# Global attention in blocks of 256 queries instead of halves of 512

## The chip, the cores and the metric

One NeuronCore of a Trainium2 chip runs the whole program, and the other cores are idle. The metric is the device time of one execution in microseconds (us). An execution works through four batches of 1024 tokens one after the other, in one hardware loop of which the body is the same for each batch. Of the engines, TensorE (PE) multiplies and transposes, VectorE (DVE) and ScalarE (ACT) do elementwise work and reductions, GpSimd (POOL) helps, and SyncE (SP) mainly issues DMAs. Every engine takes its instructions in order, and the engines meet at semaphores.

## The reference, cut to what matters

The model has two layers. The change touches only the global attention of the second one, `_L1_attn_ref`, with 1024 tokens, 16 heads and a head width of 8:

```python
Q, K, V = (proj(Wq, bq), proj(Wk, bk), proj(Wv, bv))     # 4 x 16 x 1024 x 8
logits = jnp.einsum('bhqd,bhkd->bhqk', Q, K) / scale * scale_matrix
attn = jax.nn.softmax(logits, axis=-1)
out = jnp.einsum('bhqk,bhkd->bhqd', attn, V) * (1.0 + yellow * eps_adaptive)
out = out.transpose(0, 2, 1, 3).reshape(B, S, d) @ Wo.T + bo
```

Before it stand the first layer (a kernel attention with cumulative sums and a mixture of experts), and after it a stack of two local attentions with feed-forward parts. These are the same in both kernels.

## The kernel before, in words

**Operands.** The 16 heads form four groups of four. `QS` and `KS` hold queries and keys of a group in bf16 pieces, 48 rows per head, so that a bf16 product gives nearly the fp32 product. A head of a group has a number `j = 2 s + r`: `r` says in which half of the partitions (from 0 or from 64) it lies, `s` is an index. Two products with different `r` run side by side on PE. Two further rows of `QS` (50 in all) hold the maximum of each query's scores, in two bf16 pieces, against rows of -1 in `KS`, so that the product of 50 rows gives score minus maximum.

**Two streams.** The maxima come first, from products of their own. A "maximum" is one product of 128 queries by 512 keys into one bank of PSUM (`maxima`, L1350 by the helper `mm`), which DVE reduces to a column (L1105). A half is 512 queries of one group: it has 4 query tiles x 2 key halves x 4 heads = `MPH` = 32 maxima, and there are `HALVES` = 8 halves, so 256 maxima for a batch. When the 32 of a half are done, DVE joins them to 16 columns in `mtop` (L1110), PE transposes these ("mT", L1584), ACT copies the rows to `mrw` (`rows_out`, L650), POOL splits them into two pieces `msp` (L475, L477), SP writes them to DRAM (`load_max`, L375) and, when that has landed, reads them into `QS` with two DMAs (L380).

The second stream has 128 steps `n` for a batch. Two steps make a unit of 512 queries by 128 keys; step `n` takes the pair of heads `s = n % 2`. In a step PE does two products of 128 keys by 512 queries, side by side (`st_ps`), ACT takes the exponential of 128x1024 in one instruction (L658), and three steps later PE multiplies `vaug` (values and a 1 for the denominator) with the exponentials in four products of 256 columns. These collect in bank 4. After 16 steps a half is complete, and ACT copies bank 4 to `on` (L669), at `n = 16 (h + 1) + 2` for half `h`. PE doesn't begin the next half's value products before that copy.

**How they are woven.** PE's order is written out: ahead of step `n` it issues the maxima up to number `ahead(n + 1)`, where `ahead(n) = 38 + 2 n + min(2 (n // 3), 8)`. So a step has two maxima, and four steps early on have four. The maxima and transposes share a ring of banks: all eight for the first 32, then banks 5, 6 and 7, each free again when DVE (for an mT: ACT) has read it. The transpose of half `h` stands behind the second maximum of the half after it; for the first and last half directly behind its own. At `n = 16 h` PE waits for the row of half `h` (`m_row`).

**SP's order.** SP does `load_max(h)` for h = 0 to 7. Between these it loads the operands of the groups (`load_group`) and moves the finished output of a group away (`move_out(g)`): eight DMAs of 32 KB from `on` to `o_t` and `den_t` (L387, L388), which wait for both copies to `on` of the group. `move_out(0)` stands behind `load_max(3)`, `move_out(1)` behind `load_max(5)`, `move_out(2)` ahead of `load_max(7)`. The first copy to `on` of group g waits on ACT until all eight moves of group g-1 have landed (`act.wait_ge(S["on_moved"], 128 * g)`, L668), since it writes over what they read.

Of the kernel before, what the change touches and what calls it, by code (L numbers as in the profile page):

```python
# [14 lines left out]
P = 128  # L15
# [19 lines left out]
UNITS = HALVES * T  # L35
MPH = 32
AHEAD = MPH + 6
CATCH_UP = 8
# [19 lines left out]
def build(nc, d, out):  # L58

    with ExitStack() as ctx:  # L60
# [135 lines left out]
        mxp = take([2, GH, T // 2, 2])  # L196
        mtop = take([2, MPH // 2])
# [41 lines left out]
        xa xaT_ps xaT q_ps k_ps v1_ps qkf bf1 r1 bf2 bf3 vaug scr_w0 scr_w1 qs_early qs_loaded0 qs_loaded1 qs_loaded2 qs_loaded3 mx_ps mx mtop mT_ps mrw msp m_scr m_row  # L239
# [49 lines left out]
        def max_of(h, n):  # L289

            if h == 0:
                return n // 4 % 4, n // 16, n // 2 % 2
            return n // 8, n // 2 % 2, n // 4 % 2

        def ring_bank(kind, h, n):

            i = ring_at[kind, h, n]
            return i % 8 if i < MPH else 5 + i % 3
# [6 lines left out]
        def ahead(n):  # L305

            return AHEAD + 2 * n + min(2 * (n // 3), CATCH_UP)
# [19 lines left out]
        def _(sp):  # L327
# [13 lines left out]
            with sp.Fori(0, B) as b:  # L341
# [28 lines left out]
                def load_max(h):  # L370
                    g, hq = h // 2, h % 2
                    sp.wait_ge(S["msp"], 2 * (h + 1))
                    if h >= 2:
                        sp.wait_ge(S["m_row"], 32 * h)
                    sp.dma_start(scr_m[h % 2].rearrange("i (r c) -> r i c", c=P), msp[0:MPH // 2, h % 2])\  # L375
                        .then_inc(S["m_scr"], 16)
                    sp.wait_ge(S["m_scr"], 16 * (h + 1))
                    rows = scr_m[h % 2].rearrange("i (s r n) -> r i s n", r=2, n=HALF)
                    for r in range(2):
                        sp.dma_start(QS[64 * r + STACK:64 * r + STACK + PIECES_M, g, :, HALF * hq:HALF * hq + HALF],  # L380
                                     rows[r]).then_inc(S["m_row"], 16)

                def move_out(g):
                    sp.wait_ge(S["on"], 2 * g + 2)
                    for j in range(GH):
# [56 lines left out]
        def _(pool):  # L442
            with pool.Fori(0, B) as b:
# [26 lines left out]
                for h in range(HALVES):  # L470
                    rows = slice(0, MPH // 2)
                    pool.wait_ge(S["mrw"], h + 1)
                    if h >= 2:
                        pool.wait_ge(S["m_scr"], 16 * (h - 1))
                    pool.tensor_copy(msp[rows, h % 2, 0], mrw[rows, h % 2]).then_inc(S["msp"], 1)  # L475
                    pool.wait_ge(S["msp"], 2 * h + 1)
                    pool.tensor_tensor(msp[rows, h % 2, 1], mrw[rows, h % 2], msp[rows, h % 2, 0], ALU.subtract)\  # L477
# [36 lines left out]
        def _(act):  # L514
# [18 lines left out]
            with act.Fori(0, B) as b:  # L533
# [110 lines left out]
                def rows_out(h):  # L644

                    rows = slice(0, MPH // 2)
                    act.wait_ge(S["mT_ps"], h + 1)
                    if h >= 2:
                        act.wait_ge(S["msp"], 2 * (h - 1))
                    act.copy(mrw[rows, h % 2], PS[rows, ring_bank("mT", h, 0), 0:P]).then_inc(S["mrw"], 1)  # L650

                rows_out(0)
                for n in range(2 * UNITS + 3):
                    if n < 2 * UNITS:
                        act.wait_ge(S["st_ps"], n + 1)
                        if n >= 8:
                            act.wait_ge(S["pv"], n // 2 - 3)
                        act.activation(pb[:, n % 8], pair(2 * (n % 2)), ACT.Exp).then_inc(S["p"], 1)  # L658
                        for h in range(1, HALVES):
                            last = MPH * (h + 1) + (1 if h < HALVES - 1 else -1)  # L660
                            if ahead(n) <= last < ahead(n + 1):
                                rows_out(h)
                    if n >= 16 and n % 16 == 2:
                        h = n // 16 - 1
                        g, hq = h // 2, h % 2
                        act.wait_ge(S["pv"], T * (h + 1))
# [90 lines left out]
        def _(dve):  # L757
# [128 lines left out]
            with dve.Fori(0, B) as b:  # L886
# [213 lines left out]
                for h in range(HALVES):  # L1100
                    for n in range(MPH):
                        t, hf, s = max_of(h, n)
                        j = 2 * s + n % 2
                        dve.wait_ge(S["mx_ps"], h * MPH + n + 1)
# [842 lines left out]
```

## Time and profile before

| | us |
|---|---|
| median of 3 runs | 2665.46 (2664.93 to 2665.88) |
| profiled execution, its own time | 2669.65 |
| profiled execution, span | 2667.9 |
| mean granted clock of TensorE in it | 0.913 |
| PE busy, 17520 matmuls | 2175.1 |
| DVE busy | 1967.1 |
| ACT busy | 1435.0 |
| POOL busy | 584.0 |

The profile is of one execution. Its own time is 1.75 us more than its span, for what lies around it, and 4.2 us more than the median. An engine's busy time is the sum over its instructions; for PE it is modelled, since matmuls are pipelined. A line of the view of instructions in order of time begins with the start in us from the span's start and the duration in us, then engine, line of the code, operation, output and input, and in square brackets the idle time of the engine before it and what ended it; x5 means that five such in a row are merged.
### The profile page before, as it was taken

The numbers are of one execution on the slowest core, as the hardware profiler recorded it, in microseconds if no ns is written. First come the engines' busy times: TensorE is split into PE (matmuls) and PEld (weight loads), VectorE is DVE, ScalarE is ACT, GpSimd is POOL, SyncE is SP. The second block draws the span as 40 slices with busy tenths as digits, with TensorE's granted clock in tenths as the row PEclk, the third lists the DMA queues.
The fourth block names the chain that finished last, engine by engine and source line by source line (L and its number), as shares of the span: only waits on it lengthen the run. The fifth ranks groups of instructions, "written<-read, shape, count | busy, mean of one in ns | idle before, by whom it ended". The sixth has DMA issues, their size and how long they took to land.

```text
span 2667.9 us, 46774 instructions
## 1 busy us (share of the span) xinstructions
PE 2175.1 (82%) x17520; PEld 1235.2 (46%) x17520; DVE 1967.1 (74%) x4192; ACT 1435.0 (54%) x2637; POOL 584.0 (22%) x400
## 2 busy tenths in 40 slices
PE   3799689878779959988779977997877995898777
PEld 3667312354647712246465741225564672223645
DVE  4865789678675589967777469967877657996677
ACT  1234267674733427766653335777473342776755
POOL 0062100124134200040405320004312531003050
PEclk9999779989879969999888987998987996999889
DMA  4000200011000020010100021001100003001010
GB/s 151 0 1 1 72 26 10 15 23 30 15 10 1 2 83 18 10 30 5 31 21 1 1 60 31 18 6 31 24 15 18 1 1 84 18 10 29 7 30 21
DMA packets 58920, 63.92 MB, mean 24 GB/s; under 512 B 17136, under 2 KB 44080, under 8 KB 58160
## 3 DMA queue, kind: packets, MB, share of 16 engines
q1 hardware_dynamic: 55480, 57.77, 8.6%
q8 instruction: 148, 2.42, 0.4%
q10 hardware_dynamic: 3192, 2.90, 0.3%
q14 instruction: 100, 0.82, 0.1%
HBM read 25.19 MB, written 15.01 MB: 15 GB/s over the span
## 4 chain that ended last, share of the span: by engine, by line
PE 47%; DVE 28%; ACT 14%; issue 6%; DMA 2%; SPq 2%; POOL 0%; DVEq 0%; ACTq 0%; POOLq 0%
PE PS L1350 44%; DVE arena L1105 10%; ACT arena L715 7%; DVE arena L1204 2%; ACT arena L658 1%; PE PS L1675 1%; DVE tmp L1179 1%; DVE s_at L1179 1%; DVE arena L1172 1%; PE PS L1368 1%; DMA tmp<-xf 1%; ACT tmp L669 1%; DVE arena L1291 1%; SPq L329 1%; ACT arena L723 1%
## 5 line engine op out<-in xcount | busy, mean ns | idle before, releaser
L1350 PE MATMUL PS<-arena 128*32 128x256 f32 (+4 forms) x10240 | 807.7, 349 | 132.7 <-DVE arena L1105 50.1
L1105 DVE TENSOR_REDUCE arena<-PS 128x1 f32<-128x512 f32 x1024 | 640.5, 685 | 41.1 <-PE PS L1350 41.1
L658 ACT ACTIVATE arena<-PS 128x1024 f32<-128x1024 f32 x512 | 517.9, 1028 | 174.1 <-PE PS L1350 173.0
L1350 PEld LDWEIGHTS PS<-arena 128*32 128x32 f32 (+4 forms) x10240 | 309.2, 121 | 626.0 <-DVE arena L1105 265.6
L610 ACT ACTIVATE arena<-PS 128x512 f32<-128x512 f32 x256 | 150.8, 597 | 244.2 <-PE PS L1350 244.0
L1350 PEld LDWEIGHTS PS<-w2e,arena 128*128 128x128 f32 x2048 | 246.0, 192 | 50.6 <-issue 49.8
L1350 PE MATMUL PS<-w2e,arena 128*128 128x128 f32 x2048 | 247.7, 275 | 0.3
L715 ACT ACTIVATE arena<-PS,arena 128x128 f32<-128x128 f32 x512 | 230.9, 546 | 22.3 <-DVE arena L1241 20.9
L1068 DVE TENSOR_TENSOR arena<-PS,arena 128x512 f32<-128x512 f32 x128 | 86.2, 689 | 208.5 <-PE PS L1350 208.1
L1350 PE MATMUL PS<-wqkv,arena 128*128 128x512 f32 x384 | 179.4, 607 | 25.5 <-ACT arena L697 21.7
L465 POOL TENSOR_TENSOR zz<-zz,arena 128x512 f32<-128x512 f32 x104 | 135.4, 1302 | 265.4 <-DVE arena L1068 236.6
L475 POOL CAST arena<-arena 16x128 bf16<-16x128 f32 x32 | 9.0, 280 | 699.0 <-ACT arena L650 699.0
L715 ACT ACTIVATION_READ_ACCUMULATOR arena<-PS,arena 128x1 f32 x512 | 149.7, 293 | 0.0
L454 POOL TENSOR_TENSOR arena<-arena 128x1024 f32<-128x1024 f32 x32 | 75.2, 2350 | 249.9 <-ACT arena L562 239.8
L1239 DVE TENSOR_REDUCE arena<-PS 128x8 f32<-128x1024 f32 x64 | 78.3, 1224 | 63.4 <-PE PS L1350 62.7
L502 POOL TENSOR_TENSOR tmp<-xf,b2f 128x1024 f32<-128x1024 f32 x8 | 18.8, 2355 | 471.1 <-ACT xT L735 471.1
L1350 PE MATMUL PS<-x,w1e 128*128 128x512 f32 x256 | 120.5, 596 | 0.1
L1350 PE MATMUL PS<-xT,w1e 128*128 128x512 f32 x256 | 120.5, 596 | 0.1
L1350 PEld LDWEIGHTS PS<-wqkv,arena 128*128 128x128 f32 x384 | 69.3, 193 | 104.6 <-issue 83.1
L1350 PE MATMUL PS<-xT,wf 128*128 128x512 f32 (+1 forms) x192 | 89.8, 597 | 3.8 <-ACT xT L735 3.8
L696 ACT ACTIVATE arena<-PS 128x1024 f32<-128x1024 f32 x32 | 32.8, 1024 | 103.8 <-DVE s_at L1179 103.8
L1350 PE MATMUL PS<-c_blk,arena 128*128 128x16 f32 x256 | 54.8, 374 | 41.0 <-ACT arena L523 41.0
(301 smaller groups left out, 3435.3 us busy)
## 6 DMA issues: line engine op xcount, KB each, us to landing
arena<-arena SPq DMA_DIRECT2D x120, 128.0 KB, 2.3
scr_q<-arena SPq DMA_DIRECT2D x40, 128.0 KB, 2.5
scr_k<-arena SPq DMA_DIRECT2D x40, 128.0 KB, 2.4
arena<-scr_k SPq DMA_DIRECT2D x24, 200.0 KB
arena<-scr_q SPq DMA_DIRECT2D x24, 192.0 KB
x_in<-in_x SPq DMA_DIRECT2D x5, 512.0 KB, 4.0
out_x<-tmp SPq DMA_DIRECT2D x4, 512.0 KB, 3.9
wqkv<-in_wqkv SPq DMA_DIRECT2D x1, 1536.0 KB, 7.1
```

What stands on the lines that cost most here:

```text
L454: pool.tensor_tensor(ub[:, c % 2], vsb[:, c % 2], bsb[:, c % 2], ALU.mult).then_inc(S["ub"], 1)
L465: pool.tensor_tensor(zz[:, half], src[:, half], ym[:, m % 4], ALU.add).then_inc(S["z"], 1)
L610: act.activation(hs[:, n % 8], PS[:, up_bank("up", k, c), :], ACT.Silu).then_inc(S["hs"], 1)
L658: act.activation(pb[:, n % 8], pair(2 * (n % 2)), ACT.Exp).then_inc(S["p"], 1)
L696: act.activation(qk_sq[l][t % 2], pair(2 * (t % 2)), ACT.Square).then_inc(S["sq"], 1)
L715: act.activation(pl[:, n % 3, r, c], PS[:, 2 * (n % 2) + r, KEYS * c:KEYS * c + KEYS], ACT.Exp, bias=ml[:, n % 2, r, c:c + 1], scale=rq[:, ...
L1068: dve.tensor_tensor(ym[:, m % 4], PS[:, 4 + m % 4, :].rearrange("p (t w) -> p t w", w=W), bc(comb[:, half, e // EPG, e % EPG], [P, T // 2, ...
L1105: dve.tensor_reduce(mxp[:, h % 2, j, t, hf:hf + 1], PS[:, ring_bank("mx", h, n), :], AX, ALU.max)\
L1179: ins = dve.tensor_tensor(o, v, bc(w, [P, 2, HL, DL // 2], 2), ALU.mult)
L1204: dve.tensor_reduce(ssq[:, k], qk_sq[l][k % 2].rearrange("p (h c) -> p h c", c=DL), AX, ALU.add).then_inc(S["ssq"], 1)
L1239: link(dve.tensor_reduce(ml[:, n % 2], sv, AX, ALU.max))
L1350: return pe.matmul(o, w, v, start=start, stop=stop, **kw)
```

## The change

A block of 256 queries of a group takes the place of the half. A batch has 16 blocks with 16 maxima each; number and form of the maxima are the same (256 of 128x512). The first 32 are interleaved: 16 for the first key half of blocks 0 and 1, then 8 that complete block 0, then 8 that complete block 1. Each block has its own transpose (8 columns instead of 16), copy, split and three DMAs, so 16 of each a batch instead of 8, and each block's transpose stands behind the second maximum of the block after it (only the last one directly behind its own).

A step is now one block by 128 keys for all four heads: PE does four products of 256 columns (two side by side for `s = 0`, then two for `s = 1`, all into the same two banks) instead of two products of 512 columns. ACT's exponential has the same form, and the value products are four of 256 columns as before. There are still 128 steps, and the copies to `on` stay at the same steps `n`. The run-ahead is constant: `ahead(n) = 34 + 2 n`.

On SP, `move_out` is cut in two: heads 0 and 1 of a group behind `load_max` of block 6, 10 and 13, heads 2 and 3 behind that of block 7, 11 and 14. ACT does the first two `rows_out` ahead of its first exponential. `load_group(2)` and `(3)` stand behind `load_max` of block 1 and 5. There are two semaphores `m_row0` and `m_row1` in turn.

The diff, cut to its core (constants, ring, SP, ACT, PE; in DVE's loop only the numbering and the place of L1110 follow):

```diff
-UNITS = HALVES * T
-MPH = 32
-AHEAD = MPH + 6
-CATCH_UP = 8
+BLOCKS = 2 * HALVES
+QB = HALF // 2
+STEPS = BLOCKS * T
+MPB = 2 * (QB // P) * GH
+MAXIMA = BLOCKS * MPB
+ROWS = GH * QB // P
+AHEAD = 2 * MPB + 2
...
+        def max_at(m):
+
+            if m < 2 * MPB:
+                return m // 8 % 2, m // 4 % 2, m // 2 % 2, m // MPB
+            return m // MPB, m // 8 % 2, m // 4 % 2, m // 2 % 2
+
+        def maxima_by(blk):
+
+            return (MPB + MPB // 2, 2 * MPB)[blk] if blk < 2 else MPB * (blk + 1)
+
+        def row_after(blk):
+
+            return maxima_by(blk) + (2 if blk < BLOCKS - 1 else 0)
+
+        row_at = {row_after(blk): blk for blk in range(BLOCKS)}
+
         ring = []
-        for h in range(HALVES):
-            for n in range(MPH):
-                ring.append(("mx", h, n))
-                if n == 1 and 2 <= h:
-                    ring.append(("mT", h - 1, 0))
-            if h == 0 or h == HALVES - 1:
-                ring.append(("mT", h, 0))
+        for m in range(MAXIMA):
+            ring.append(("mx", m))
+            if m + 1 in row_at:
+                ring.append(("mT", row_at[m + 1]))
...
         def ahead(n):
 
-            return AHEAD + 2 * n + min(2 * (n // 3), CATCH_UP)
+            return AHEAD + 2 * n
...
-                for h in range(HALVES):
-                    if h == HALVES - 1:
-                        move_out(NGRP - 2)
-                    load_max(h)
-                    if h in (0, 2):
-                        load_group(2 + h // 2)
-                    if h >= 3 and h % 2 == 1 and h < HALVES - 1:
-                        move_out((h - 3) // 2)
+                for blk in range(BLOCKS):
+                    load_max(blk)
+                    if blk in (1, 5):
+                        load_group(2 + blk // 4)
+                    if blk in (6, 10, 13):
+                        move_out((blk - 6) // 3, (0, 1))
+                    if blk in (7, 11, 14):
+                        move_out((blk - 7) // 3, (2, 3))
...
                 rows_out(0)
-                for n in range(2 * UNITS + 3):
-                    if n < 2 * UNITS:
+                rows_out(1)
+                for n in range(STEPS + 3):
+                    if n < STEPS:
                         act.wait_ge(S["st_ps"], n + 1)
                         if n >= 8:
-                            act.wait_ge(S["pv"], n // 2 - 3)
+                            act.wait_ge(S["pv"], n - 7)
                         act.activation(pb[:, n % 8], pair(2 * (n % 2)), ACT.Exp).then_inc(S["p"], 1)
-                        for h in range(1, HALVES):
-                            last = MPH * (h + 1) + (1 if h < HALVES - 1 else -1)
-                            if ahead(n) <= last < ahead(n + 1):
-                                rows_out(h)
+                        if ahead(n + 1) in row_at:
+                            rows_out(row_at[ahead(n + 1)])
...
-                        for r in range(2):
-                            rows = slice(64 * r, 64 * r + STACK + PIECES_M)
-                            ins = mm(PS[:, 2 * (n % 2) + r, :], KS[rows, g, st, P * kt:P * kt + P],
-                                     QS[rows, g, st, HALF * hq:HALF * hq + HALF], tile_position=(64 * r, 0))
+                        for s in range(2):
+                            for r in range(2):
+                                rows = slice(64 * r, 64 * r + STACK + PIECES_M)
+                                ins = mm(PS[:, 2 * (n % 2) + r, QB * s:QB * s + QB], KS[rows, g, s, P * kt:P * kt + P],
+                                         QS[rows, g, s, QB * q4:QB * q4 + QB], tile_position=(64 * r, 0),
+                                         skip_group_check=True)
                         ins.then_inc(S["st_ps"], 1)
```

## Rows read from the trace of the kernel before

**Rows 1.** The page: span, busy engines, chain that ended last.

```profile
span 2667.9 us, 46774 instructions
...
PE 2175.1 (82%) x17520; PEld 1235.2 (46%) x17520; DVE 1967.1 (74%) x4192; ACT 1435.0 (54%) x2637; POOL 584.0 (22%) x400
...
PE 47%; DVE 28%; ACT 14%; issue 6%; DMA 2%; SPq 2%; POOL 0%; DVEq 0%; ACTq 0%; POOLq 0%
```

**Rows 2.** Busy time by stretch, batch 1: the stage, then its even middle.

```profile
955.20:1153.60 198.40, 164.42 (x1557) 44.30 (x1556) 170.26 (x271) 135.09 (x146) 5.62 (x17) 0.91 0.11 27
...
989.30:1125.20 135.90, 120.53 (x1206) 31.84 (x1202) 129.85 (x212) 104.63 (x112) 4.19 (x12) 1.00 0.07 14
```

**Rows 3.** DVE in order of time, one half's maxima in the even middle.

```profile
403.21 0.19 DVE L1110 TENSOR_REDUCE arena<-arena 128x16 f32<-128x32 f32 x1
403.31 1.28 DVE L1105 TENSOR_REDUCE arena<-PS 128x1 f32<-128x512 f32 x2
405.15 12.52 DVE L1105 TENSOR_REDUCE arena<-PS 128x1 f32<-128x512 f32 x20 [0.56 <-PE PS L1350]
418.00 6.28 DVE L1105 TENSOR_REDUCE arena<-PS 128x1 f32<-128x512 f32 x10 [0.34 <-PE PS L1350]
424.32 0.19 DVE L1110 TENSOR_REDUCE arena<-arena 128x16 f32<-128x32 f32 x1
```

**Rows 4.** DVE, then ACT, in order of time: how batch 1 begins.

```profile
969.63 4.86 DVE L1105 TENSOR_REDUCE arena<-PS 128x1 f32<-128x512 f32 x8
974.52 0.18 DVE L1110 TENSOR_REDUCE arena<-arena 128x16 f32<-128x32 f32 x1
975.80 1.29 DVE L1105 TENSOR_REDUCE arena<-PS 128x1 f32<-128x512 f32 x2 [1.09 <-PE PS L1350]
...
981.04 2.06 ACT L658 ACTIVATE arena<-PS 128x1024 f32<-128x1024 f32 x2 [4.22 <-PE PS L1350]
...
988.42 1.02 ACT L658 ACTIVATE arena<-PS 128x1024 f32<-128x1024 f32 x1 [0.96 <-PE PS L1350]
```

**Rows 5.** PE, then ACT, in order of time, batch 1, behind the last maximum.

```profile
1125.56 0.27 PE L1584 MATMUL PS<-ident,arena 128*16 128x128 f32 x1 [1.67 <-DVE arena L1110]
...
1129.45 6.52 ACT L658 ACTIVATE arena<-PS 128x1024 f32<-128x1024 f32 x7 [0.48 <-PE PS L1350]
```

**Rows 6.** Busy time by stretch, batch 1, behind the last transpose.

```profile
1125.80:1129.20 3.40, 3.40 (x23) 0.67 (x22) 0.77 (x1) 2.18 (x3) 0.70 (x2) 0.50 0.00 0
```

**Rows 7.** DVE, ACT, then SP in order of time, batch 0, behind half 5.

```profile
445.43 0.19 DVE L1110 TENSOR_REDUCE arena<-arena 128x16 f32<-128x32 f32 x1
...
450.10 1.02 ACT L658 ACTIVATE arena<-PS 128x1024 f32<-128x1024 f32 x1 [0.22 <-PE PS L1350]
...
458.82 0.59 ACT L669 COPY tmp<-PS 128x512 f32<-128x512 f32 x1 [0.21 <-DMA tmp<-tmp]
...
448.43 0.31 SPq L375 DMA_DIRECT2D scr_m<-arena  x1
449.77 1.22 SPq L380 DMA_DIRECT2D arena<-scr_m  x2
451.03 0.68 SPq L387 DMA_DIRECT2D xT<-tmp  x1
...
453.12 0.62 SPq L388 DMA_DIRECT2D tmp<-tmp  x1
...
455.79 1.24 SPq L388 DMA_DIRECT2D tmp<-tmp  x1
```

**Rows 8.** SP's own waits in batch 0's stage: total, times, longest, in us.

```profile
SPq L380 <- DMA scr_m<-arena: 11.9, 8, 2.9
```

**Rows 9.** Weight port and PE in order of time, at the start of one step.

```profile
380.34 0.14 PEld L1350 LDWEIGHTS PS<-arena 48*128 48x128 bf16 x4 [0.52 <-DVE arena L1105]
380.37 0.61 PE L1350 MATMUL PS<-arena 48*128 48x512 bf16 x4
```

**Rows 10.** Groups of weight loads, batch 0's stage: those of the scores.

```profile
L1350 PEld LDWEIGHTS PS<-arena 50*128 50x128 bf16 x256 | 13.6, 95 | 11.2 <-ACT arena L658 7.4 <-issue 2.1 <-DMA arena<-scr_m 0.8
```

More of the change, by code:

```diff
@@ L368, in load_group, with load_max, move_out @@
                             .then_inc(S["qs_loaded%d" % g], 16)
[L370 to L378, printed above, removed]
+                def load_max(blk):
+                    g, q4 = blk // 4, blk % 4
+                    sp.wait_ge(S["msp"], 2 * (blk + 1))
+                    if blk >= 2:
+                        sp.wait_ge(S["m_row%d" % ((blk - 1) % 2)], 32 * ((blk + 1) // 2))
+                    maxes = scr_m[blk % 2][:, 0:GH * QB]
+                    sp.dma_start(maxes.rearrange("i (r c) -> r i c", c=P), msp[0:ROWS, blk % 2]).then_inc(S["m_scr"], 16)
+                    sp.wait_ge(S["m_scr"], 16 * (blk + 1))
+                    rows = maxes.rearrange("i (s r n) -> r i s n", r=2, n=QB)
                     for r in range(2):
-                        sp.dma_start(QS[64 * r + STACK:64 * r + STACK + PIECES_M, g, :, HALF * hq:HALF * hq + HALF],
-                                     rows[r]).then_inc(S["m_row"], 16)
-                def move_out(g):
+                        sp.dma_start(QS[64 * r + STACK:64 * r + STACK + PIECES_M, g, :, QB * q4:QB * q4 + QB],
+                                     rows[r]).then_inc(S["m_row%d" % (blk % 2)], 16)
+                def move_out(g, heads):
                     sp.wait_ge(S["on"], 2 * g + 2)
-                    for j in range(GH):
+                    for j in heads:
                         h = GH * g + j
@@ L468, in _ @@
                 pool.tensor_tensor(s1[:], xa[:], bc(res["bo"][:], [P, T, W], 1), ALU.add).then_inc(S["xab"], 1)
[L470 to L477, printed above, removed]
+                for blk in range(BLOCKS):
+                    rows = slice(0, ROWS)
+                    pool.wait_ge(S["mrw"], blk + 1)
+                    if blk >= 2:
+                        pool.wait_ge(S["m_scr"], 16 * (blk - 1))
+                    pool.tensor_copy(msp[rows, blk % 2, 0], mrw[rows, blk % 2]).then_inc(S["msp"], 1)
+                    pool.wait_ge(S["msp"], 2 * blk + 1)
+                    pool.tensor_tensor(msp[rows, blk % 2, 1], mrw[rows, blk % 2], msp[rows, blk % 2, 0], ALU.subtract)\
                         .then_inc(S["msp"], 1)
@@ L1553, in ring_free @@
                     if ring_last[i]:
-                        kind, h, n = ring_last[i]
-                        if kind == "mx":
-                            pe.wait_ge(S["mx"], MPH * h + n + 1)
-                        else:
-                            pe.wait_ge(S["mrw"], h + 1)
-                def maxima(lo, hi):
-                    for m in range(lo, min(hi, MPH * HALVES), 2):
-                        h, n = m // MPH, m % MPH
-                        g, hq = h // 2, h % 2
-                        t, hf, s = max_of(h, n)
-                        if h == 0 and n == 0:
+                        kind, n = ring_last[i]
@@ L1567, in maxima @@
+                        pe.wait_ge(S["mx" if kind == "mx" else "mrw"], n + 1)
+                def maxima(lo, hi):
+                    for m in range(lo, min(hi, MAXIMA), 2):
+                        blk, t, s, hf = max_at(m)
+                        g, q4 = blk // 4, blk % 4
+                        if m == 0:
                             pe.wait_ge(S["qs_early"], 16 * 4)
-                        if h == 0 and n == MPH // 2:
+                        if m == MPB:
                             pe.wait_ge(S["qs_loaded0"], 16 * 4)
-                        if n == 0 and hq == 0 and h:
+                        if m and m % (4 * MPB) == 0:
@@ L1605, in _ @@
                 maxima(0, ahead(0))
-                for n in range(2 * UNITS + 3):
-                    if n < 2 * UNITS:
-                        u, st = n // 2, n % 2
-                        h, kt = u // T, u % T
-                        g, hq = h // 2, h % 2
+                for n in range(STEPS + 3):
+                    if n < STEPS:
+                        blk, kt = n // T, n % T
+                        g, q4 = blk // 4, blk % 4
                         maxima(ahead(n), ahead(n + 1))
-                        if n % 16 == 0:
-                            pe.wait_ge(S["m_row"], 32 * (h + 1))
+                        if kt == 0:
+                            pe.wait_ge(S["m_row%d" % (blk % 2)], 32 * (blk // 2 + 1))
@@ new lines, in _ @@
+                        blk, k = (n - 3) // T, (n - 3) % T
+                        pe.wait_ge(S["p"], n - 2)
+                        if k == 0 and blk % 2 == 0 and blk:
+                            pe.wait_ge(S["on"], blk // 2)
+                        c0 = QB * (blk % 2)
+                        for j in range(GH):
+                            c = HALF * (j % 2) + QB * (j // 2)
+                            ins = mm(PS[32 * j:32 * j + 32, 4, c0:c0 + QB], vaug[:, k, GH * (blk // 4) + j],
+                                     pb[:, (n - 3) % 8, c:c + QB], start=(k == 0), stop=(k == T - 1),
+                                     tile_position=(0, 32 * j), skip_group_check=True)
@@ L1640, in _ @@
+                        ins.then_inc(S["pv"], 1)
                 pe.wait_ge(S["p"], NGRP * T * GH)
```

95 lines of the change are left out of this document (39 added, 56 removed).

## The prediction

> **What bounds the kernel now.** I read the page first. PE is busy 82% of the span and DVE 74%, and the chain that ended last is shared, 47% on PE and 28% on DVE [rows 1]: no one engine bounds the program, so the stage must be read by itself. The view by stretch gives the global attention of batch 1: 198.4 us, with DVE busy 170.3, PE 164.4 and ACT 135.1 [rows 2]. Four such stages are 0.3 of the span. In the order of time DVE runs its reductions without a gap for 20 in a row, 12.52 us or 0.626 each [rows 3]. So the even middle goes at DVE's pace, two maxima and one step in 1.25 us. ACT confirms it: its exponential takes 1.02 and it idles 0.22 before it [rows 7]; the weight port waits 0.52 for a reduction to free a bank [rows 9]. The stage has three parts with three limits:
>
> - The beginning. A row of maxima must be complete before the first exponential. From the join (L1110) at 974.52 to the first exponential at 981.04 are 6.5 us [rows 4]. PE is at half clock until 989.3: from there the granted clock is 1.00, and the beginning puts the stage's mean at 0.91 [rows 2]. A step with value products takes 1.02 + 0.96 = 1.98 us [rows 4]: PE bounds.
> - The middle, bound by DVE. One half takes 424.32 - 403.21 = 21.11 us, of which 32 x 0.626 = 20.03 are reductions. Of the other 1.08, 0.34 is an idle time at the copy to `on`, which leaves 0.74 for join and transpose (0.56 of it idle) [rows 3].
> - The end. `ahead` reaches 256 at n = 105, so the maxima are all issued with step 104, and 24 steps go without them, bound by ACT: 6.52 / 7 = 0.93 us a step [rows 5].
>
> So a change gains in the middle only if DVE loses fewer microseconds.
>
> **The change, part by part, for one batch.**
>
> *The earlier first row.* Block 0 is complete after 24 maxima, 8 sooner. Eight take 4.86 us [rows 4], so its join is at about 969.7 on batch 1's clock, and its row is there by 975.5. But PE's order puts the transpose of block 1 ahead of step 0, and that needs 32 maxima. DVE has by then paid one more gap (1.09 is the row [rows 4]; 0.7, since two maxima stand behind the transpose here) and goes at the cold pace of 1.45 us a pair (from 975.80, two reductions and 0.17 idle), so the 32nd ends at 976.0, the 34th at 977.4, and the first exponential comes at about 978.7: 2.3 us sooner. ACT's table load moves behind the second `rows_out` and still ends before that.
>
> *The run-ahead without catch-up.* The early steps of before have four maxima at times, which keeps DVE busier while PE is cold. Followed pair by pair, the new kernel has issued 46 maxima where the old has issued 48 (986.4), though it is two steps further, and 54 against 54 at 991 to 992. So DVE's progress is the same, and the earlier start buys nothing at the end. I take 0, within 1.3 us (one pair) either way. It holds if the clock rises no later after the start than now.
>
> *More rows.* The middle has 13 transposes (blocks 2 to 14) for 6 (halves 1 to 6). Seven more at 0.74 [rows 3] are **+5.2 us**. Their geometry is the same: two maxima behind the block's last, ACT's copy behind the step's exponential. Bounds: 0.18 each if only the join remains (+1.3), 1.1 each as at the start (+7.7) [rows 4]. Each row now has nine steps from transpose to use instead of seven, so no row is late. The halved DMAs on SP fit between blocks that are 10 us apart.
>
> *The shorter end.* `ahead` is 256 at n = 111, so 18 steps instead of 24 go without maxima: 6 x 0.93 [rows 5] = **-5.6 us**. DVE's total is what it was, so that is a true gain. What DVE does behind the last row is asked for by PE only at n = 125, 14 steps later.
>
> *Four products for two.* PE streams the same columns, with two more weight loads a step. Their mean is 95 ns [rows 10]. Cost from below: nothing. From above: both exposed, 0.19 a step. Four loads, the two of the maxima and the two of the scores on the same partitions, pass in 0.14 us while the products that began at 380.37 still run [rows 9]. So I take hidden, 0.02 us on 12 cold steps, +0.2. The cover is PE's own idle time, (135.90 - 120.53) / 99 = 0.155 us a step in the middle [rows 2]; without it the excess counts 105 times.
> The Trainium skill (TensorE: Matmul & The Clock Gate, Part 3) says that a weight load overlaps running matmuls "only when row_grp differs"; the same page (Part 2) allows it for the background buffer too. The strict rule would expose the second pair; rows 9 speak against it.
>
> *The moves of the output.* This is the part that decides. The first copy to `on` of groups 1, 2 and 3 (n = 50, 82, 114) waits on ACT for all eight moves of the group before. Now four of these stand behind `load_max` of block 7, 11 and 14. The transpose of block 7 is issued in step 47 (34 + 2 x 47 = 128, and 130 is its place), that of block 11 in step 79, that of block 14 in step 103. So for groups 1 and 2 ACT needs the moves three steps after the transpose; for group 3 there are eleven steps, enough. Before, it was some nine steps, and even so the copy at 458.82 waited 0.21 us [rows 7].
> The time is in rows 7, with the join at 445.43 as zero. SP issues the write of the row at +3.00, the reads at +4.34, the first move at +5.60 and the fourth at +7.69. The last move lands and frees ACT 458.82 - 455.79 = 3.0 us after its issue begins (less the 0.6 by which that issue was held up: 2.4). So ACT is freed at +10.1 to +10.7. It would have copied behind the exponential of step 50, the third after the transpose's own: 450.10 and the pace of 0.93 [rows 5] give +5.60. The wait is 4.5 to 5.1 us; I take **4.6**, as a half's moves hold each other up less. Queued behind it on ACT is the exponential of step 51, and PE waits for the copy before the value products of step 51, with DVE's next maxima behind these. DVE has at most three banks and idles already at each copy [rows 3], so all of the wait passes to it, and the run-ahead, tied to n, never makes it up. Two a batch, eight in all: 8 x 4.6 = **+37 us**.
> Two additions. The write of the row takes up to 2.9 us to land instead of about 1.0 (8 waits sum to 11.9, so two of eight are long [rows 8]): two of the eight stalls are 1.9 longer, +4. And PE idles about 5 us in each. Ahead of the last transpose PE idled 1.7 us in batch 1 [rows 5], and then its clock was 0.50 for 3.4 us [rows 6]. A cold step costs 1.98 for 1.25, so 3.4 us of half clock cost 1.3 and twice that 2.5: I take 1.5 each, +12, from 0 to +20.
> [...]
>
> **The sum.** Beginning 0, rows +5.2, end -5.6, products +0.2: about 0 a batch, 0 in four. Stalls 37 + 4 + 12 = 53. The profiled execution would go from 2669.65 to about 2722; it stands 4.2 above the median, so the median goes from 2665.5 to **2718 us**. 0.2% or 5.3 us is about what a measurement of this kernel can tell from no change.
>
> **The rivals.**
>
> - *The moves arrive in time.* That needs 4.5 us less than rows 7 give for the same DMAs in the same order, or SP running ahead of the row, which its waits forbid. Then the sum is 0 and the time 2665, within 6. Against it also: the old order had three times the room and was just in time.
> - *Faster, by transposes that cost little.* If the joins fall into gaps that DVE has anyway, only 1.3 of 5.2 us remain a batch: 4 x -3.9 = -16, 2650. It decides only if the stalls together are under 16 us, 2 us each, less than half of the lowest bound. The lead in the exponentials (2.3 us) speaks for it, DVE's unbroken runs [rows 3] against.
> - *PE becomes the bound.* If the second pair of weight loads is exposed at 0.19 us a step, 0.155 is covered in the middle and 0.035 is not, x 105 = 3.7, and 0.19 x some 15 cold steps = 2.9; with the end's 18 steps partly touched, some 8 us a batch, +32: 2750.
> - *The stalls are shorter, the clock holds.* 8 x 4.0 and no additions: 2697.
>
> **Chances.** The forecast with its spread (2697 to 2748) 0.80; PE the bound 0.08 (on top of the stalls); in time 0.05; faster 0.03; something else slower 0.04. The range from below is 32 us of stalls less 4 for the beginnings, 2694; from above it is 8 x 5.1 + 15 (every write long) + 20 + 6 = 82, 2748. Slower by over 0.2% holds 0.92, within 0.2% 0.05, faster 0.03.
>
> **What would show each step right or wrong.** The copy L669 of the third and fifth half in each batch would show an idle time of 4 to 7 us ended by a DMA `tmp<-tmp`, and DVE an idle time of about 5 at the same place; the half that holds it lasts some 28 us from join to join instead of 21.9. Plain halves would last 21.9 (two joins). The first exponential would come some 2.7 us after block 1's join. The last maximum of a batch would end 5 + 13 us later than now, and 18 exponentials would follow it. Granted clock under 1.00 behind each stall would show the clock's part. Wrong would be: no wait at these copies, a steady step over 1.25 us (products), or a weight port that idles on "issue".

## The result, and the profile after

The changed kernel takes 2716.06 us (median of 4 runs, 2713.98 to 2717.45) against 2665.67 for the kernel before (4 runs, 2664.93 to 2666.13). The ratio is 1.0189, with a 95% interval from 1.0171 to 1.0206: 50 us or 1.9% slower. The profiled execution has a span of 2714.7 us against 2667.9, so 46.8 us more.

The page of the changed kernel, span, busy time, chain that ended last, and two groups of instructions; below them the same two groups of the kernel before:

```profile
span 2714.7 us, 49306 instructions
...
PE 2197.8 (81%) x18576; PEld 1287.8 (47%) x18576; DVE 1974.4 (73%) x4224; ACT 1443.1 (53%) x2669; POOL 605.8 (22%) x464
...
PE 44%; DVE 33%; ACT 12%; issue 6%; DMA 2%; SPq 2%; POOL 0%; DVEq 0%; ACTq 0%; POOLq 0%
...
L1113 DVE TENSOR_REDUCE arena<-PS 128x1 f32<-128x512 f32 x1024 | 644.0, 686 | 97.0 <-PE PS L1359 97.0
L669 ACT ACTIVATE arena<-PS 128x1024 f32<-128x1024 f32 x512 | 520.8, 1027 | 176.2 <-PE PS L1359 173.4
```

```profile
L1105 DVE TENSOR_REDUCE arena<-PS 128x1 f32<-128x512 f32 x1024 | 640.5, 685 | 41.1 <-PE PS L1350 41.1
L658 ACT ACTIVATE arena<-PS 128x1024 f32<-128x1024 f32 x512 | 517.9, 1028 | 174.1 <-PE PS L1350 173.0
```

DVE's work grew by 7 us only [rows 1]. What grew is its idle time ahead of the reductions: 97.0 us, where the kernel before has 41.1 in the same group. That is 56 us more of waiting for PE, in an engine that sets the pace of the middle.

The list of ACT's waits shows what made PE late. Total us, times and the longest, of the changed kernel and then of the kernel before:

```profile
ACT tmp L678 <- DMA tmp<-tmp: 28.3, 8, 3.6
...
ACT tmp L669 <- DMA tmp<-tmp: 0.9, 3, 0.4
```

Eight times a copy to `on` waits some 3.5 us for a move of the output, twice a batch. One of them, batch 1, in order of time: ACT, then DVE, then SP.

```profile
1050.29 1.02 ACT L669 ACTIVATE arena<-PS 128x1024 f32<-128x1024 f32 x1 [1.01 <-PE PS L1359]
1051.21 0.24 ACT L660 COPY arena<-PS 8x128 f32<-8x128 f32 x1
...
1053.99 1.02 ACT L669 ACTIVATE arena<-PS 128x1024 f32<-128x1024 f32 x1 [0.23 <-PE PS L1359]
1058.56 0.59 ACT L678 COPY tmp<-PS 128x512 f32<-128x512 f32 x1 [3.55 <-DMA tmp<-tmp]
1059.05 1.03 ACT L669 ACTIVATE arena<-PS 128x1024 f32<-128x1024 f32 x1
1061.38 1.02 ACT L669 ACTIVATE arena<-PS 128x1024 f32<-128x1024 f32 x1 [1.30 <-PE PS L1359]
1063.36 1.02 ACT L669 ACTIVATE arena<-PS 128x1024 f32<-128x1024 f32 x1 [0.96 <-PE PS L1359]
...
1049.34 0.17 DVE L1119 TENSOR_REDUCE arena<-arena 128x8 f32<-128x16 f32 x1
...
1060.95 1.29 DVE L1113 TENSOR_REDUCE arena<-PS 128x1 f32<-128x512 f32 x2 [4.66 <-PE PS L1359]
1062.93 1.29 DVE L1113 TENSOR_REDUCE arena<-PS 128x1 f32<-128x512 f32 x2 [0.69 <-PE PS L1359]
...
1052.31 0.27 SPq L386 DMA_DIRECT2D scr_m<-arena  x1
1053.51 0.53 SPq L390 DMA_DIRECT2D arena<-scr_m  x2
1054.09 0.64 SPq L397 DMA_DIRECT2D xT<-tmp  x1
...
1056.12 0.62 SPq L398 DMA_DIRECT2D tmp<-tmp  x1
```

This answers [rows 7]. The join of block 7 is at 1049.34, and ACT copies its rows at 1051.21. SP writes them at +2.97 and reads them at +4.17, and issues the four late moves from +4.75 to +6.78. They have landed at +9.2, but ACT was ready to copy at +5.7. DVE, with nothing left in its banks, idles 4.66 us. Behind the wait the exponentials come 2.33 and then 1.98 us apart, and not 1.25. The busy time by stretch goes with it: PE was idle for most of one stretch of 3.4 us, and the granted clock is half there and in the stretch behind it (the columns are as in [rows 2]).

```profile
1056.60:1060.00 3.40, 0.71 (x8) 0.23 (x8) 0.00 (x0) 1.44 (x2) 0.00 (x0) 0.51 0.13 19
1060.00:1063.50 3.50, 3.50 (x28) 0.98 (x28) 1.86 (x3) 1.24 (x3) 0.00 (x0) 0.50 0.02 5
```

The beginning and the plain middle of the changed kernel, DVE and ACT of batch 1:

```profile
975.64 0.17 DVE L1119 TENSOR_REDUCE arena<-arena 128x8 f32<-128x16 f32 x1
...
982.07 0.17 DVE L1119 TENSOR_REDUCE arena<-arena 128x8 f32<-128x16 f32 x1
...
984.71 1.02 ACT L669 ACTIVATE arena<-PS 128x1024 f32<-128x1024 f32 x1 [0.37 <-PE PS L1359]
...
1116.19 0.17 DVE L1119 TENSOR_REDUCE arena<-arena 128x8 f32<-128x16 f32 x1
...
1118.11 8.78 DVE L1113 TENSOR_REDUCE arena<-PS 128x1 f32<-128x512 f32 x14 [0.56 <-PE PS L1359]
1126.92 0.17 DVE L1119 TENSOR_REDUCE arena<-arena 128x8 f32<-128x16 f32 x1
```

The first exponential follows block 1's join by 2.6 us. A block without a copy to `on` takes 1126.92 - 1116.19 = 10.73 us; the 0.56 behind each join is the same as in [rows 3], and it now comes every block.

### The profile page after: what moved, and what is told of

It is laid out like the page before. It is cut to its first block, busy times and chain, and to the rows that moved or that the text cites. A ratio compares the mean times of both kernels' runs of the same rounds, so it can differ in the third digit from the quotient of the medians.

```text
span 2714.7 us, 49306 instructions
## 1 busy us (share of the span) xinstructions
PE 2197.8 (81%) x18576; PEld 1287.8 (47%) x18576; DVE 1974.4 (73%) x4224; ACT 1443.1 (53%) x2669; POOL 605.8 (22%) x464
## 4 chain that ended last, share of the span: by engine, by line
PE 44%; DVE 33%; ACT 12%; issue 6%; DMA 2%; SPq 2%; POOL 0%; DVEq 0%; ACTq 0%; POOLq 0%
PE PS L1359 40%; DVE arena L1113 14%; ACT arena L724 7%; DVE arena L1213 2%; PE PS L1678 1%; DVE s_at L1188 1%; DVE arena L1181 1%; PE PS L1377 1%; DMA tmp<-xf 1%; DVE tmp L1188 1%; ACT tmp L678 1%; DMA tmp<-tmp 1%; DVE arena L1300 1%; SPq L339 1%; ACT x_in L738 1%
## 5 line engine op out<-in xcount | busy, mean ns | idle before, releaser
L1359 PE MATMUL PS<-arena 128*32 128x256 f32 (+4 forms) x11264 | 822.3, 336 | 158.1 <-DVE arena L1113 53.0
L1359 PEld LDWEIGHTS PS<-arena 128*32 128x32 f32 (+4 forms) x11264 | 359.6, 120 | 610.2 <-DVE arena L1113 250.2
L1359 PE MATMUL PS<-wqkv,arena 128*128 128x512 f32 x384 | 182.8, 617 | 25.5 <-ACT arena L706 21.7
L485 POOL CAST arena<-arena 8x128 bf16<-8x128 f32 x64 | 17.9, 279 | 737.3 <-ACT arena L660 737.3
```

The source lines that it names most:

```text
L1359: return pe.matmul(o, w, v, start=start, stop=stop, **kw)
```

## The experiments

The theory: the loss is the place of the late moves, in two parts, the wait and the clock behind it, and all else cancels. The rival: the smaller blocks cost it (products of 256 columns, twice the rows).

| kernel | us (median) | ratio to before, 95% interval |
|---|---|---|
| changed kernel | 2716.1 | 1.0189 (1.0171 to 1.0206) |
| changed, all moves early | 2665.3 | 0.9997 (0.9989 to 1.0006) |
| changed, two late moves | 2701.6 | 1.0140 (1.0123 to 1.0158) |
| changed, PE kept busy in the wait | 2695.2 | 1.0115 (1.0093 to 1.0136) |
| before, late moves alone | 2704.6 | 1.0152 (1.0133 to 1.0171) |
| before, products of 256 columns alone | 2666.7 | 0.9999 (0.9990 to 1.0007) |

**All moves early.** One edit takes the suspected cause out of the changed kernel:

```diff
                     if blk in (6, 10, 13):
-                        move_out((blk - 6) // 3, (0, 1))
-                    if blk in (7, 11, 14):
-                        move_out((blk - 7) // 3, (2, 3))
+                        move_out((blk - 6) // 3, (0, 1, 2, 3))
```

> The changed kernel with all eight moves of groups 0 and 1 behind the maxima row of block 6 and 10 (those of group 2 behind block 13), nothing else altered. Theory (the late moves are the whole loss): in the changed kernel a step that holds a stalled copy takes 5.06 us for 1.39, and the cold steps behind it add 1.3 to 2.7, together some 5.0 to 6.3 a stall, 46 us for eight; without them 2716 - 46 = about 2670 us, no idle time ended by a DMA at the copy L678, every step pair of blocks 21.9 us from join to join, clock 1.00 from the start's end to the last join. Rival (the smaller blocks cost it: 256-column products, twice the rows): 2705 or more, with long steps left. Rival (faster than before by the shorter end): 2655 or less.

Measured: 2665.3 us, the time of before. All 50 us of the loss are gone, a little more than the 46 expected. The same copy in this kernel, ACT of batch 1, has no idle time ahead of it, and the next steps keep their pace:

```profile
1041.47 1.02 ACT L667 ACTIVATE arena<-PS 128x1024 f32<-128x1024 f32 x1 [0.22 <-PE PS L1357]
1042.39 0.58 ACT L676 COPY tmp<-PS 128x512 f32<-128x512 f32 x1
1042.86 1.04 ACT L667 ACTIVATE arena<-PS 128x1024 f32<-128x1024 f32 x1
1044.34 1.02 ACT L667 ACTIVATE arena<-PS 128x1024 f32<-128x1024 f32 x1 [0.44 <-PE PS L1357]
```

So the blocks of 256 as such cost and gain nothing in sum.

**Late moves alone, in the kernel before.** The other direction: halves of 512 stay, and only the last four moves are held back.

```diff
                 def move_out(g):
                     sp.wait_ge(S["on"], 2 * g + 2)
                     for j in range(GH):
+                        if j == 2 and g < 2:
+                            sp.wait_ge(S["p"], 32 * g + 50)
```

> The kernel before, halves of 512 as they were, with one part alone of the change: the last four moves of groups 0 and 1 wait on SP for the exponential of step 49 and 81, so that they are about as late against the copy as in the changed kernel. Theory: the copies of the third and fifth half idle 3.0 to 3.5 us for a DMA, and with cold steps behind them each costs about 5.5 us: 2665.7 + 44 = about 2710 us. Rival (the late moves cost little by themselves, since PE could catch up, and blocks cost): under 2680.

Measured: 2704.6 us, 39 more than before; eight copies wait 25.5 us in all, 3.2 each. The wait for the move in batch 1:

```profile
1058.92 0.59 ACT L671 COPY tmp<-PS 128x512 f32<-128x512 f32 x1 [3.12 <-DMA tmp<-tmp]
```

The loss comes with the late moves, whatever the block. By the medians it is 4.9 us a stall where I expected 5.5. Step by step, the profile has 5.8 a stall (46 us in all, against the steps of the kernel before with split products, further down), while its parts outside the attention took 8 us less than there (1556.6 for 1564.7); why is open.

**Two late moves instead of four.**

```diff
-                        move_out((blk - 6) // 3, (0, 1))
+                        move_out((blk - 6) // 3, (0, 1, 2))
...
-                        move_out((blk - 7) // 3, (2, 3))
+                        move_out((blk - 7) // 3, (3,))
```

> The changed kernel with two late moves instead of four for groups 0 and 1 (heads 0 to 2 behind block 6 and 10, head 3 behind block 7 and 11). Theory (the wait is set by when the last move lands): two moves fewer, issued 0.67 us apart, make the wait 3.5 - 1.3 = 2.2 us instead of 3.5, eight times, and the clock falls as after the longer wait or a little less: 2716 - 11 to 2716 - 20, about 2702 us. Rival (the wait is for block 7's row chain or for something else than the moves): still 3.5 us and 2716.

Measured: 2701.6 us. The eight waits are 17.4 us in all, 2.2 each, as expected from two issues less:

```profile
1056.99 0.59 ACT L678 COPY tmp<-PS 128x512 f32<-128x512 f32 x1 [2.21 <-DMA tmp<-tmp]
```

The wait follows the number of DMAs ahead of the last landing. 1.4 us less wait a stall (28.3 less 17.4, by eight) went with 14.5 / 8 = 1.8 us less in the median.

**PE kept busy in the wait.** Twelve products of which the output is overwritten, ahead of PE's wait for the copy:

```diff
                         if k == 0 and blk % 2 == 0 and blk:
+                            if blk in (6, 10):
+                                pe.wait_ge(S["p"], n)
+                                for i in range(12):
+                                    mm(PS[:, 2 * ((n + 1) % 2), :], QS[0:STACK, blk // 4, 0, 0:P],
+                                       KS[0:STACK, blk // 4, 0, 0:HALF], tile_position=(0, 0), skip_group_check=True)
                             pe.wait_ge(S["on"], blk // 2)
```

> The changed kernel with twelve idle products of 512 columns on PE in each of the eight stalls (2.6 us at full clock; their output is overwritten), ahead of PE's wait for the copy to on. The wait of ACT for the moves stays. Theory (the stall has two parts, the wait and the clock): the copy still idles 3.5 us for the DMA, but the clock stays at 1.00 behind it, so the steps behind take 1.25 to 1.48 us instead of 1.98 to 2.34: 1.3 to 2.7 us less a stall, 2716 - 17 = 2699 us. Rival (the clock is not the cause of the long steps behind, or falls all the same): 2714 to 2722.

Measured: 2695.2 us, 21 less than the changed kernel with the same waits (28.2 us in all). The steps behind one of them in batch 1, ACT, and then the stretches from the wait on:

```profile
1055.79 0.58 ACT L678 COPY tmp<-PS 128x512 f32<-128x512 f32 x1 [3.49 <-DMA tmp<-tmp]
1056.27 1.03 ACT L669 ACTIVATE arena<-PS 128x1024 f32<-128x1024 f32 x1
1057.65 1.02 ACT L669 ACTIVATE arena<-PS 128x1024 f32<-128x1024 f32 x1 [0.35 <-PE PS L1359]
1059.62 1.02 ACT L669 ACTIVATE arena<-PS 128x1024 f32<-128x1024 f32 x1 [0.95 <-PE PS L1359]
...
1052.00:1055.40 3.40, 3.18 (x18) 1.18 (x14) 1.57 (x3) 0.29 (x1) 0.00 (x0) 1.00 0.28 43
1055.40:1058.80 3.40, 2.38 (x24) 0.70 (x26) 1.29 (x2) 2.54 (x3) 0.00 (x0) 0.82 0.00 0
1058.80:1062.20 3.40, 3.31 (x30) 0.90 (x26) 2.33 (x4) 1.84 (x2) 0.00 (x0) 0.68 0.00 0
```

The first step behind the copy takes 1.38 us where it took 2.33. But the clock still fell, only later and for a shorter time, so I was wrong that it would stay at 1.00.

The size came out, and yet not where I looked for it. Take each step behind the eight waits against the same step of the early-moves kernel: the changed kernel loses 17.2 us there, and this one 10.1. So filling the wait gave back 7 us behind the stalls, 0.9 a stall. The two profiled spans differ by 20. Another 8 us lie between the last maximum of a batch and its last exponential, 87.8 us in four batches against 80.0. There the time goes with the granted clock: a batch's end takes 19.7 us at a mean of 1.00, 21.0 at 0.92 and 22.3 at 0.85. Three of the changed kernel's four are of the longest kind, three of this kernel's of the shortest, and three of the early-moves kernel's of the middle one. Some 6 us more lie outside the attention (1560.1 for 1566.1), where both kernels have the same instructions. Why filling the eight waits goes with a higher clock so far behind them is not shown. So the clock is a cause of its own behind the stalls, but 2.6 us a stall (21 / 8) would put down to it what lies elsewhere.

**Products of 256 columns alone, in the kernel before.**

```diff
-                        for r in range(2):
-                            rows = slice(64 * r, 64 * r + STACK + PIECES_M)
-                            ins = mm(PS[:, 2 * (n % 2) + r, :], KS[rows, g, st, P * kt:P * kt + P],
-                                     QS[rows, g, st, HALF * hq:HALF * hq + HALF], tile_position=(64 * r, 0))
+                        for i in range(2):
+                            for r in range(2):
+                                rows = slice(64 * r, 64 * r + STACK + PIECES_M)
+                                q0 = HALF * hq + HALF // 2 * i
+                                ins = mm(PS[:, 2 * (n % 2) + r, HALF // 2 * i:HALF // 2 * i + HALF // 2],
+                                         KS[rows, g, st, P * kt:P * kt + P], QS[rows, g, st, q0:q0 + HALF // 2],
+                                         tile_position=(64 * r, 0), skip_group_check=True)
```

> The kernel before with each score product of 512 columns cut into two of 256 (four a step instead of two, with four weight loads), nothing else. Theory (the second pair of loads is hidden behind running products): within 2 us of before, steady step 1.25 us. Rival (loads wait for products on the same partitions): 0.1 to 0.19 us on the cold steps and 0.035 on the others, 2680 or more.

Measured: 2666.7 us, no difference. The loads double and keep their length (512 at 96 ns, for 256 at 95 in [rows 10]), and the steps stay 1.25 apart:

```profile
L1350 PEld LDWEIGHTS PS<-arena 50*128 50x128 bf16 x512 | 25.2, 96 | 22.3 <-ACT arena L658 6.6 <-issue 5.0 <-DMA arena<-scr_m 0.8
```

**What would be better.** With the stalls gone, blocks of 256 stand level with halves. The early-moves kernel is the base of the next runs, save where the kernel before is named.

*A run-ahead of 28.* Block 0's row needs only 26 maxima, so step 0 can go before block 1's transpose:

```diff
-AHEAD = 2 * MPB + 2
+AHEAD = MPB + MPB // 2 + 4
...
-                rows_out(1)
```

> The changed kernel with all moves behind block 6, 10 and 13, and a run-ahead of 28 instead of 34: step 0 no longer waits for the transpose of block 1, and three steps fewer go without maxima. Theory: the end is 3 x 0.93 = 2.8 us shorter a batch, the first exponential comes 2.5 us sooner, but cold steps with value products begin with fewer maxima behind DVE, which costs one to two pairs (1.2 to 2.5 us): 0 to -1.6 us a batch, 2659 to 2666. Rival (each row is needed six steps behind its transpose, 7.5 us, too tight for the chain of DMAs): a wait of the scores for the row's DMA at each block, slower than 2670.

Measured: 2654.8 us, ratio 0.9962 (0.9948 to 0.9977). It gained 10.5 us against the base, more than the 6 I allowed. In batch 1 the first exponential comes 19.7 us behind the first maximum instead of 23.5, though PE waits 1.0 us for the first row's DMA. From the first maximum to the last it takes 1.2 us longer (176.6 for 175.4), and 17.7 instead of 21.0 us pass from the last maximum to the end. No other row is waited for.

*The transpose behind its step, and a wait for each bank.* PE issues a block's transpose only ahead of the next pair of maxima, when the join is long done, ACT copies its rows ahead of that step's exponential, and PE waits for each bank by itself:

```diff
-                        for r in range(2):
-                            ring_free(ring_at["mx", m + r])
+                        if row_at.get(m, 0) >= 2:
+                            turn(row_at[m])
                         q0 = QB * q4 + P * t
                         for r in range(2):
+                            ring_free(ring_at["mx", m + r])
                             rows = slice(64 * r, 64 * r + STACK)
...
+                        if 2 <= row_at.get(ahead(n), 0) < BLOCKS - 1:
+                            rows_out(row_at[ahead(n)])
                         act.wait_ge(S["st_ps"], n + 1)
```

(`turn(k)` is the transpose with its two waits, as it was.)

> The changed kernel with all moves behind block 6, 10 and 13 and, for blocks 2 to 14, the transpose issued behind the scores and value products of its step instead of ahead of them, ACT's copy of the rows ahead of the exponential, and PE waiting for each maximum's bank by itself instead of for both of a pair. Theory (the 0.74 us per row are PE waiting for the join, then both banks of the ring being waited for): a block goes from 10.9 us to 10.2 to 10.6, a batch loses 4 to 9 us, and the time is 2630 to 2650 us. Rival (the cost is DVE's own: join and the empty ring slot): 2662 to 2668.

Measured: 2629.6 us, ratio 0.9863 (0.9844 to 0.9882), just under the expected 2630 to 2650. DVE in batch 1:

```profile
1036.99 0.17 DVE L1119 TENSOR_REDUCE arena<-arena 128x8 f32<-128x16 f32 x1
1037.08 2.48 DVE L1113 TENSOR_REDUCE arena<-PS 128x1 f32<-128x512 f32 x4
1039.95 7.26 DVE L1113 TENSOR_REDUCE arena<-PS 128x1 f32<-128x512 f32 x12 [0.39 <-PE PS L1359]
1047.25 0.17 DVE L1119 TENSOR_REDUCE arena<-arena 128x8 f32<-128x16 f32 x1
```

A block takes 10.26 us, 0.47 less than in the changed kernel. The idle time went from 0.56 to 0.39. Twelve reductions take 7.26, and the last of them has its own 0.68 in that, so they start (7.26 - 0.68) / 11 = 0.598 us apart; the twenty of [rows 3] start (12.52 - 0.68) / 19 = 0.623 apart. So two things changed, and the next two runs separate them.

*The bank waits alone.* In the early-moves kernel, and in the kernel before:

```diff
-                        for r in range(2):
-                            ring_free(ring_at["mx", h, n + r])
                         q0 = HALF * hq + P * t
                         for r in range(2):
+                            ring_free(ring_at["mx", h, n + r])
                             rows = slice(64 * r, 64 * r + STACK)
```

> The changed kernel with all moves behind block 6, 10 and 13, and PE waiting for each maximum's bank by itself; transposes and copies of rows stand where they stood. Theory (the reductions ran 0.626 us apart because each pair of products came just as DVE was done, and 0.597 with the product there sooner): 0.029 us for each of some 210 maxima of the middle, 6 us a batch, 2666 - 24 = 2642 us, and the last 12 us come from the transposes' place. Rival (all 36 us come from the transposes' place): 2666.

> The kernel before, halves of 512, with PE waiting for each maximum's bank by itself, nothing else. Theory: as in the run above, 0.029 us for some 200 maxima a batch: 2666 - 23 = 2643 us, reductions of the middle 0.597 apart. Rival (the pace of 0.626 is DVE's own in this kernel): 2666.

Measured: 2638.8 us, ratio 0.9899 (0.9883 to 0.9916), and 2639.8, ratio 0.9907 (0.9890 to 0.9924). In the kernel before with this one edit sixteen reductions follow each other like this:

```profile
1052.76 9.66 DVE L1105 TENSOR_REDUCE arena<-PS 128x1 f32<-128x512 f32 x16 [0.47 <-PE PS L1350]
```

They start (9.66 - 0.68) / 15 = 0.599 us apart, as expected (0.597), and the idle time behind the join is 0.47 for 0.56. So of the 36 us, 26.5 come from the bank waits and 9 from the place of the transposes and of ACT's copies. Of these 9, the blocks of the middle show 0.07 us each, some 4 in all: 10.33 us with the bank waits alone (no copy to `on` in them), 10.26 with both.

*All together*, with a run-ahead of 28 and of 30:

> The kernel with the transposes behind the step and waits for each maximum's bank by itself, and a run-ahead of 28 as in the run before. Theory (the two gains lie in different parts, one in the middle and one at beginning and end): 2630 - 11 = 2619 us. Rival (a row is now needed five steps, 6.0 us, behind its transpose, and the chain of copy, split, write and read takes 5.2 or more): scores wait for the row's DMA at each block, and the gain is lost: 2626 or more.

> The same with a run-ahead of 30, six steps from transpose to use. Theory: 2630 - 7 = 2623 us without any wait for a row. If 28 waits for its rows, this one is the faster of the two.

Measured: 2614.6 us for 28, ratio 0.9815 (0.9799 to 0.9831), where 2619 was expected, and 2626.4 for 30, ratio 0.9855 (0.9839 to 0.9872), where 2623 was. The kernel with 28 beats both kernels of this study, the one before by 50 us. Its gain of 50.7 us on the early-moves kernel is 4.5 more than its two parts gave alone (10.5 and 35.7), which is within the intervals; that it is faster than 30 is clear of them. The joins show where. With 28 they are 10.25 us apart from the third on, in all but two cases, and whether a copy to `on` lies between them or not; with 30 they are 10.3 and 10.8 in turn, the longer one with the copy in it. With 28 the copy comes in the step before a transpose, so the idle times of both seem to fall together. That was not tested by itself, and it takes more than the 28: in the kernel with a run-ahead of 28 and the old waits, the blocks with a copy take 11.29 us and the others 10.73.

The rival came true only in part. No row is late in the middle, but PE waits for the first row of each batch, 1.8 to 2.0 us with 28 and 0.6 to 0.8 with 30. And the moves are on the edge again. In batch 1 one pair of joins is 12.83 us apart, where ACT waits for a move:

```profile
ACT tmp L677 <- DMA tmp<-tmp: 1.4, 1, 1.4
```

DVE of the kernel with 28, two joins with a copy to `on` between them:

```profile
1045.30 0.17 DVE L1118 TENSOR_REDUCE arena<-arena 128x8 f32<-128x16 f32 x1
1045.39 2.47 DVE L1112 TENSOR_REDUCE arena<-PS 128x1 f32<-128x512 f32 x4
1048.26 7.26 DVE L1112 TENSOR_REDUCE arena<-PS 128x1 f32<-128x512 f32 x12 [0.40 <-PE PS L1358]
1055.55 0.17 DVE L1118 TENSOR_REDUCE arena<-arena 128x8 f32<-128x16 f32 x1
```

## Why the prediction was right, point by point

- **The moves.** Forecast: two stalls a batch at the copies of the third and fifth half, 4.6 us each and 37 in all. There are eight, and ACT waits 28.3 us, 3.54 each. The step that holds one takes 5.06 us for 1.39, so 3.67 are lost a stall, 29 in all. The mechanism was right and this term too large by 8; each stall came out under the lowest bound of 4.5. The chain was taken from the old DMAs, and the new ones for a row are half the size. Its two reads into `QS` take SP 0.53 us and not 1.22, and the write has landed 1.20 behind its issue instead of 1.34. So the moves are issued 0.9 us sooner behind the join than in [rows 7].
- **The slow writes.** Forecast +4, measured 0: none of the eight stalls had one.
- **The clock.** Forecast +12, with 0 to +20. The steps behind a stall lose 1.2 to 2.7 us, 17 in all, so this term was too small by 5. Another 5 us, forecast by no term, lie behind the last maxima (87.8 us in four batches, 82.7 in the early-moves kernel), at a lower granted clock there.
- **The sum.** 53 forecast, 50 measured by the medians. In the profile the stalls and the steps behind them are 46 of these. The stalls and the writes were 12 too many, the clock 5 to 10 too few: that the total comes within 3 us is partly luck. The mechanism is not luck.
- **The range.** It is stated as 2697 to 2748, and worked out as 2694 to 2748: 32 less 4 on 2665.5 is 2694. The result lies in both.
- **More rows, shorter end.** The early-moves kernel shows them without the stalls. From the first maximum to the last there are 175.4 us in batch 1 for 169.9 before: +5.5 for +5.2. From the last maximum to the last exponential's end there are 21.0 for 26.5: -5.5 for -5.6. They cancel as forecast. The lengths are batch 1's; batch 0 of the kernel before took 175.2 to its last maximum, for a slower start.
- **The beginning.** The first exponential came 2.2 us sooner after the first maximum (2.3 forecast), and as forecast it bought nothing at the end. The other signs came true too: 2.6 us from block 1's join to it, two plain blocks in 21.9 us, and 27.6 with a stall.
- **The products.** Forecast hidden; alone in the old kernel 0.9999 (0.9990 to 1.0007).
- **The rivals.** In time: no. Faster by cheap transposes: no, each cost its 0.56 of idle time again. PE the bound: no, the products alone cost nothing. Shorter stalls with a clock that holds: the stalls were shorter still than its 4.0, but the clock fell behind each of them.
- **Group 3's copy** (n = 114) was forecast to find its moves landed, and no wait stands there.
- One reading stands corrected, and it moves no term by more than half a microsecond a batch. 0.626 us is the length of a run over its count, with the last reduction's full 0.68 in it; they start 0.623 apart. And I took that for DVE's own pace. It was the pace of DVE and PE passing banks to each other; with another order of waits it is 0.598.

## What to carry to other kernels

When a step is cut into smaller ones, list for each transfer the step it is issued behind and the step that needs it. The work was the same here, but four moves went from nine steps ahead of their use to three. From the join ACT was ready after 5.7 us, while the chain of DMAs took 9.2 (in [rows 7] the two were 13.2 and 13.4), and with what the clock cost behind it that was the whole loss. Here the engine that sets the pace has a fixed run-ahead and never made up a stall, so the price was its length times its count, plus what PE's clock cost. And a pair of waits ahead of a pair of instructions delays the first for the second's sake: putting each wait ahead of its own instruction gave 1% in the early-moves kernel and in the kernel before.

## What the runs showed of the hardware that I had not expected

- Reductions of 128x512 from PSUM, which each take 0.68 us in the profile, start every 0.598 us (7.26 or 9.66 us for 12 or 16 in a row) when PE waits for each bank by itself, and every 0.623 (12.52 us for 20) when it waits for two banks at once. In neither case does the profile show idle time between them, so an unbroken row of one engine doesn't prove that the engine is alone the bound.
- Two weight loads more in each step of PE cost nothing that could be measured (0.9999, 0.9990 to 1.0007) where the products on the same partitions have 256 columns. The Trainium skill (TensorE: Matmul & The Clock Gate, Part 3) lets a load overlap only products on other partitions; the runs here agree with the page's other sentence, of a background buffer (Part 2).
- Twelve products in the wait, which made PE busy for 3.18 of 3.4 us, moved the fall of the granted clock and shortened it, but didn't prevent it: 1.00, then 0.82 and 0.68 over the next stretches. PE was idle for 1.0 us of the second of these stretches. The steps behind the eight stalls lost 10.1 us in this kernel and 17.2 in the changed one.
- At a batch's end the same instructions take 19.7, 21.0 or 22.3 us, with a mean granted clock of 1.00, 0.92 or 0.85. So in this program a few microseconds between two kernels can lie where nothing was changed, and a gain is best looked for step by step.
